# Attention of a fused block: half of the heads' probabilities transposed by DMA instead of TensorE, row transposes in their own PSUM bank, layernorm steps in other slots

## What is computed

```python
x = x + jnp.tanh(g_xattn[0]) * _L0_xattn_ref(_layernorm(x, axis=-1), ctx_1024, Wq, Wk, Wv, Wo, bo)
x = x + jnp.tanh(g_ffn[0]) * _L0_ffn_ref(_layernorm(x, axis=-1), router_w, w_gate, ...)
```

```python
scores = jnp.einsum('bhqd,bhkd->bhqk', q, k) * SCALE
scores = jnp.where(causal[None, None, :, :], scores, -jnp.inf)
probs = jax.nn.softmax(scores, axis=-1)
y = jnp.einsum('bhqk,bhkd->bhqd', probs, v)
```

## Time and profile before

| | us |
|---|---|
| median of 3 runs | 1925.9 (1924.12 to 1927.26) |
| the profiled execution | 1926.66 |
| its span in the trace | 1924.9 |
| attention, start of the span to the first expert matmul | 662.8 |
| experts | 1262.1 |

### The profile page before, as it was taken

One profiled execution on the slowest core, in us unless ns is written; L12 is line 12 of the kernel. 1 busy time (PEld: TensorE's weight loads), 2 busy tenths in 40 slices (PEclk: granted clock), 3 DMA queues, 4 the chain that ended last, 5 costly groups with the idle time before them and its releaser, 6 DMA issues.

```text
span 1924.9 us, 33464 instructions
## 1 busy us (share of the span) xinstructions
PE 1872.5 (97%) x11664; PEld 1588.0 (82%) x11664; DVE 1513.8 (79%) x3345; ACT 970.2 (50%) x2284; POOL 698.4 (36%) x939
## 2 busy tenths in 40 slices
PE   6999999999999899999999999999999999999999
PEld 6899998889999678888878888877888887888887
DVE  5888888888888887777788777787777778877776
ACT  4777777777777744243343333353334334423332
POOL 3132233232233533334433344353334453333330
PEclk9999999999999899999999999999999999999999
DMA  7565556656566231221123212114122112312111
GB/s 213 124 148 132 148 147 144 156 128 160 149 146 162 67 121 44 77 77 46 54 75 112 74 58 67 55 33 147 51 77 67 55 56 66 112 53 65 45 44 44
DMA packets 151494, 182.81 MB, mean 95 GB/s; under 512 B 11424, under 2 KB 115872, under 8 KB 151328
## 3 DMA queue, kind: packets, MB, share of 16 engines
q1 hardware_dynamic: 151328, 180.68, 33.4%
HBM read 111.43 MB, written 18.87 MB: 68 GB/s over the span
## 4 chain that ended last, share of the span: by engine, by line
PE 75%; DVE 13%; issue 5%; ACT 3%; POOL 3%; SPq 1%; DMA 1%; DVEq 0%; POOLq 0%; ACTq 0%
PE gate_up L1234 31%; PE down L1748 18%; PE bank L741 14%; PE probs_t L872 3%; PE scores L842 2%; DVE ops_lo L1091 2%; DVE acc L1599 2%; PE bank L731 1%; POOL hidden L1447 1%; DVE probs L673 1%; PE y L861 1%; PE y L859 1%; PE down L1727 1%; SPq L353 1%; DVE pt_lo L705 1%
## 5 line engine op out<-in xcount | busy, mean ns | idle before, releaser
L1234 PE MATMUL gate_up<-xo_hi,ops_hi 128*128 128x512 f32 x1120 | 440.0, 393 | 13.2 <-DVE hidden L1210 4.4
L1234 PE MATMUL gate_up<-xo_lo,ops_hi 128*128 128x512 f32 x1120 | 436.1, 389 | 0.0
L1234 PE MATMUL gate_up<-xo_hi,ops_lo 128*128 128x512 f32 x1120 | 436.1, 389 | 0.0
L1234 PEld LDWEIGHTS gate_up<-xo_hi,ops_hi 128*128 128x128 f32 x1120 | 210.2, 188 | 67.2 <-DVE gated L1210 9.6
L1599 DVE SCALAR_TENSOR_TENSOR acc<-down,scale,acc 128x512 f32<-128x512 f32 x320 | 238.1, 745 | 34.8 <-PE down L1748 34.4
L1748 PE MATMUL down<-d_hi,h_hi 128*128 128x512 f32 x640 | 249.1, 389 | 0.0
L1748 PE MATMUL down<-d_hi,h_lo 128*128 128x512 f32 x640 | 249.0, 389 | 0.0
L1748 PE MATMUL down<-d_lo,h_hi 128*128 128x512 f32 x640 | 249.0, 389 | 0.0
L1234 PEld LDWEIGHTS gate_up<-xo_lo,ops_hi 128*128 128x128 f32 x1120 | 210.2, 188 | 44.3
L1234 PEld LDWEIGHTS gate_up<-xo_hi,ops_lo 128*128 128x128 f32 x1120 | 210.3, 188 | 42.3
L1447 POOL TENSOR_TENSOR hidden<-hidden,gated 128x512 f32<-128x512 f32 x120 | 157.4, 1319 | 189.8 <-DVE hidden L1215 170.4
(11 more groups left out here) (179 smaller groups left out, 4586.2 us busy)
## 6 DMA issues: line engine op xcount, KB each, us to landing
g_raw<-in_w_gate SPq DMA_DIRECT2D x40, 512.0 KB, 3.9
u_raw<-in_w_up SPq DMA_DIRECT2D x40, 512.0 KB, 3.9
d_raw<-in_w_down SPq DMA_DIRECT2D x40, 512.0 KB, 3.7
k_stack<-k_hi SPq DMA_DIRECT2D x128, 128.0 KB, 2.6
q_stack<-q_hi SPq DMA_DIRECT2D x128, 128.0 KB, 2.6
c_in<-in_ctx_t SPq DMA_DIRECT2D x16, 512.0 KB, 3.8
x_in<-in_x SPq DMA_DIRECT2D x16, 512.0 KB, 3.8
k_stack<-k_lo SPq DMA_DIRECT2D x64, 128.0 KB, 2.6
```

Of the source, the lines that this page charges most:

```text
L1234: ins = pe.matmul(gu_ps[bank][:], ops[x][:, which, a, c, :], xo[y][:, b, c, :], start=(begins and c == 0 and i == 0), stop=(c == CH - 1 an ...
```

## The change

- Of each batch the even heads (`by_dma`) are no longer transposed by PE. ACT rounds their `probs` to float16 in SBUF (`halves[.., 0]`), POOL subtracts for the remainder (`halves[.., 1]`), both one slot behind the scores, and SP issues, two slots behind, one DMA that transposes all six 128x128 blocks into `turned`, a ring of four. The odd heads go through PE, ACT and DVE as before, three slots behind and through one bank; their results are written to `turned` too. The product with V is six slots behind instead of four.
- The scores' first matmul (queries 0 to 127) takes 128 keys instead of 256. The stacks lie in another order in SBUF, so that each of the 24 DMAs writes 4 KB in one piece instead of four of 1 KB.
- The bank set free, `rows_ps`, takes all row transposes. Those of y no longer wait for `q_lo`. The hat tile is transposed at once in slot 13 and evacuated once (`keep_hat`) instead of in four pieces.
- The layernorm steps stand in other slots (`LN_SLOT` 5 to 7, `XN_SLOT` 13 to 10, `MOMENTS_SLOT` 3 to 0, `STD_SLOT` 4 to 2). SP walks over slots as well: its loads, the stack DMAs (three in each of slots 5 to 12) and the turns are interleaved, and the store of x1 is issued in slot 0 of the next iteration.

```diff
-        return sb(f"q_stack{i}", [P, H, S], F32R), sb(f"k_stack{i}", [P, H, S], F32R)
+        return sb(f"q_stack{i}", [P, JH, C, S], F32R), sb(f"k_stack{i}", [P, JH, C, S], F32R)
...
-    RING = 4
+    RING, TURNED = 4, 4
     probs = [sb(f"probs{i}", [P, 3 * P]) for i in range(RING)]
-    pt_hi = [sb(f"pt_hi{i}", [P, 3 * P], F16) for i in range(2)]
-    pt_lo = [sb(f"pt_lo{i}", [P, 3 * P], F16) for i in range(2)]
+    halves = [sb(f"halves{i}", [P, 2, 3 * P], F16) for i in range(2)]
+    turned = [sb(f"turned{i}", [P, 2, 3, P], F16) for i in range(TURNED)]
...
-    sc_ps = [psum(f"scores{i}", [P, T, S]) for i in range(2)]
-    pt_ps = [psum(f"probs_t{i}", [P, D]) for i in range(2)]
+    sc_ps = [psum(f"scores{i}", [P, P + 3 * P]) for i in range(2)]
+    pt_ps = psum("probs_t", [P, D])
+    rows_ps = psum("rows_t", [P, D])
...
-    TR_LAG, PV_LAG = 2, 4
+    SPLIT_LAG, TURN_LAG, TR_LAG, PV_LAG = 1, 2, 3, 6
     GROUP_LAG = PV_LAG + JH
-    BANK_A, BANK_B = 0, 1
+    RES_LOAD, X_LOAD, C_LOAD, ROWS_LOAD = 2, 3, 14, 14
+    K_STACK, Q_STACK = (5, 6, 7, 8), (9, 10, 11, 12)
     K_SLOTS, K_EVAC = (0, 1, 2, 3), (2, 4)
-    X_SLOTS, X_EVAC, X_BANKS = (0, 2), (1, 3), (BANK_B, BANK_A)
+    X_SLOTS, X_EVAC = (0, 2), (1, 3)
     Q_SLOTS, Q_EVAC = (4, 5, 6, 7), (6, 8)
     V_SLOTS, V_EVAC, V_SPLIT = ((8, 9), (10, 11)), (10, 12), (11, 13)
-    Y_SLOTS, Y_EVAC, Y_BANKS = (8, 10), (9, 11), (BANK_B, BANK_A)
+    Y_SLOTS, Y_EVAC = (8, 10), (9, 11)
     O_SLOTS, O_EVAC = ((12, 13), (14, 15)), (14, 15)
-    LN_SLOT, C_SLOT, XN_SLOT = 5, 12, 13
-    RES_SLOT, MOMENTS_SLOT, STD_SLOT, HAT_SLOT = 6, 3, 4, 6
-    HAT_FIRST, HAT_T_SLOT = 4, H - C
+    LN_SLOT, C_SLOT, XN_SLOT = 7, 12, 10
+    RES_SLOT, MOMENTS_SLOT, STD_SLOT, HAT_SLOT = 6, 0, 2, 6
+    HAT_FIRST, HAT_T_SLOT, HAT_T_EVAC = 4, 13, 14
...
+    def scores_of(k, t):
+
+        return sc_ps[k % 2][:, P:2 * P] if t == 0 else sc_ps[k % 2][:, 2 * P:]
+
...
+            def turn(k):
+                wait(sp, pv_done, k - TURNED + 1)
+                sp.sem_inc(sp_passed, 1)
+                sp.wait_ge(p_lo_made, k // 2 + 1)
+                sp.dma_start(turned[k % TURNED][:].rearrange("p x t q -> p (x t) q"), halves[k // 2 % 2][:].rearrange("p x k -> p (x k)"),
+                             transpose=True).then_inc(p_turned[k // 2 % 2], DMA)
...
+                for s in range(H):
+                    if (bh := lagging(i, s, TURN_LAG)) and by_dma(bh[1]):
+                        turn(head(*bh))
+                    if s == 0 and has(i, -2):
+                        sp.wait_ge(x1_made, (i + -2).times(T, T))
+                        sp.dma_start(row(x1_v, i + -2), x_res[:]).then_inc(x1_stored, DMA)
...
+                    if s == RES_LOAD and has(i, -1):
+                        wait(sp, x1_stored, o.times(DMA))
+                        sp.dma_start(x_res[:], row(x_v, o)).then_inc(res_loaded, DMA)
+                    if s == ROWS_LOAD and hat_tile(i + 1) is not None:
+                        rows_again(hat_tile(i + 1))
+                    if s == X_LOAD and has(i, 2):
+                        sp.wait_ge(xt_done, ln.times(T))
+                        sp.dma_start(x_in[:], row(x_v, ln)).then_inc(x_loaded, DMA)
...
+                    if s in Q_STACK and has(i, 1):
+                        j = Q_STACK.index(s)
+                        if j == 0:
+                            sp.wait_ge(q_lo_made, n.times(2, 2))
                         stack(q_stack[par], j, 0, q_hi).then_inc(stacked[par][j], DMA)
                         stack(q_stack[par], j, 1, q_lo).then_inc(stacked[par][j], DMA)
                         stack(q_stack[par], j, 2, q_hi).then_inc(stacked[par][j], DMA)
...
+                    if s == C_LOAD and has(i, 3):
+                        sp.wait_ge(c_lo_made, far.times(1))
+                        sp.dma_start(c_in[:], row(c_v, far)).then_inc(c_loaded, DMA)
...
+                    if (bh := lagging(i, s, SPLIT_LAG)) and by_dma(bh[1]):
+                        k = head(*bh)
+                        m = k // 2
+                        pool.wait_ge(p_hi_made, m + 1)
+                        pool.tensor_tensor(halves[m % 2][:, 1, :], probs[k % RING][:], halves[m % 2][:, 0, :],
+                                           ALU.subtract).then_inc(p_lo_made, 1)
...
+                    if (bh := lagging(i, s, SPLIT_LAG)) and by_dma(bh[1]):
+                        k = head(*bh)
+                        m = k // 2
+                        if m >= 2:
+                            act.wait_ge(p_turned[m % 2], DMA * (m // 2))
+                        act.wait_ge(probs_made, k + 1)
+                        act.copy(halves[m % 2][:, 0, :], probs[k % RING][:]).then_inc(p_hi_made, 1)
+                    if (bh := lagging(i, s, TR_LAG)) and not by_dma(bh[1]):
+                        k = head(*bh)
+                        act.wait_ge(pt_done, k // 2 + 1)
+                        wait(act, pv_done, k - TURNED + 1)
+                        act.copy(turned[k % TURNED][:, 0].rearrange("p t q -> p (t q)"), pt_ps[:, 0:3 * P]).then_inc(pt_hi_made, 1)
...
-                        wait(dve, pt_done, i.times(H, s - RING + 1))
+                        k = head(i, s)
+                        if k >= RING and by_dma(k):
+                            dve.wait_ge(p_lo_made, (k - RING) // 2 + 1)
+                        elif k >= RING:
+                            dve.wait_ge(pt_done, (k - RING) // 2 + 1)
...
+                    if (bh := lagging(i, s, TR_LAG)) and not by_dma(bh[1]):
+                        k = head(*bh)
+                        dve.wait_ge(pt_hi_made, k // 2 + 1)
+                        p_hi, p_lo = (turned[k % TURNED][:, x].rearrange("p t q -> p (t q)") for x in range(2))
+                        dve.tensor_tensor(p_lo, pt_ps[:, 0:3 * P], p_hi, ALU.subtract).then_inc(pt_lo_made, 1)
...
-                        if has(i, 1) and t == 0:
-                            pe.wait_ge(q_lo_made, n.times(2, 2))
-                        elif has(i, 1):
-                            pe.wait_ge(v_rest_made, n.times(T, 1))
-                        else:
-                            wait(pe, x1_made, o.times(T, (0, 1 - T)[t]))
-                        transpose_rows(lambda c: y_chunk(o, t, c), bank[Y_BANKS[t]]).then_inc(yt_done, 1)
+                        if is_end(i):
+                            pe.wait_ge(x1_made, o.times(T, (0, 1 - T)[t]))
+                        elif t == 1:
+                            pe.wait_ge(yt_lo_made, o.times(T, 1))
+                        transpose_rows(lambda c: y_chunk(o, t, c), y_bank(i, t)).then_inc(yt_done, 1)
...
-                        wait(pe, max_made, i.times(H, s - 1))
+                        wait(pe, max_made, head(i, s) - 1)
                         pairs = slice(0, 3 * DH)
                         for t in range(T):
-                            ins = pe.matmul(sc_ps[s % 2][:, t, :], q_stack[par][pairs, s, tile(t)],
-                                            k_stack[par][pairs, s, :], start=True, stop=True)
+                            keys = slice(0, P * (t + 1))
+                            ins = pe.matmul(scores_of(head(i, s), t), q_stack[par][pairs, s % JH, s // JH, tile(t)],
+                                            k_stack[par][pairs, s % JH, s // JH, keys], start=True, stop=True)
...
-                        pe.wait_ge(pt_lo_made, b.times(H, h + 1))
+                        n_head = head(b, h)
+                        if by_dma(n_head):
+                            pe.wait_ge(p_turned[n_head // 2 % 2], DMA * (n_head // 4 + 1))
+                        else:
+                            pe.wait_ge(pt_lo_made, n_head // 2 + 1)
+                        p_hi, p_lo = turned[n_head % TURNED][:, 0], turned[n_head % TURNED][:, 1]
...
+                    if (bh := lagging(i, s, TR_LAG)) and not by_dma(bh[1]):
+                        j = head(*bh)
+                        pe.wait_ge(probs_made, j + 1)
+                        wait(pe, pt_lo_made, j // 2)
                         for k in range(3):
-                            ins = pe.transpose(pt_ps[h % 2][:, tile(k)], probs[h % RING][:, tile(k)], ident[:])
+                            ins = pe.transpose(pt_ps[:, tile(k)], probs[j % RING][:, tile(k)], ident[:])
                         ins.then_inc(pt_done, 1)
                     units(i, s)
+                    if s == HAT_T_SLOT and hat_tile(i) is not None:
+                        k = hat_tile(i)
+                        pe.wait_ge(x_hat_made, k + 1)
+                        transpose_rows(lambda c: x_hat[:, k % T, c * P:(c + 1) * P], rows_ps).then_inc(hat_t_done, 1)
```

179 lines of the change are left out of this document (81 added, 98 removed).

## The result

The changed kernel takes **1907.0 us** (median of 4 runs, 1905.8 to 1910.3) against 1925.3 us before (4 runs, 1924.1 to 1927.3): a ratio of 0.990, 95% interval 0.989 to 0.992. It is 18 us faster where 39 were forecast; 1907.0 lies inside the range. The profiled execution took 1910.3 us, with a span of 1908.6.

A forecast was written before the change was run, and what follows sets the result against it. PE was taken to bound the kernel, busy 97% of the span. Five batches by 2.54, eight hat batches by 3.64 and 1.2 for batch 0, less 4 at the end, give 39.0 us: 1887 us, range 1866 to 1944.

The forecast's parts named there:

- The transposes: On PE, removing three transposes for each of 8 heads saves 0.28 us each, 2.24 us a batch.
- the sum: All terms added over the whole kernel: 39.0 us gained from 1926.66, giving 1887 us as median.
- The narrower scores: On PE, a 128-column first score matmul saves 0.02 us a head, 0.3 us a batch (1.0 gained to 1.8 lost).
- the best case: Narrow score matmul on PE costs half of one with 256 columns, 0.06 us; 1.0 us gained a batch.
- The rival "dear": Narrow score matmuls cost 0.23 us each on PE, a batch loses 1.8 us, about 1920 us; chance 0.15.
- The bank of its own: Row transpose of y no longer waits on PE for q_lo: 1.1 us saved in each of eight hat batches.
- all fit into 35.6 and are priced at nothing: DVE 29.5, ACT 29.2, POOL 18 us (21 with hat tile) fit a 35.6 us batch, so cost nothing.
- The hat batches: Batches 4 to 11, with a hat tile: 3.64 us gained in each of eight, 29.1 us in all.
- The queue: On SP, a turn's issue takes 1 to 1.5 us; SP sets the pace only from 2.25 us.
- the heavy rival: A turn holds SP for 3.7 us, 47.2 us of issues a batch, 2050 us in all; chance 0.20.
- the 2.56 that were given: Issue time in us per turn on SP from which the kernel is slower than before.
- The end: Batches 14 and 15: POOL's remainders queue behind its wait for x_t; 4 us lost (gain 3 to loss 12).

The follow-up runs named there:

- h4: f2 with the first score matmul of each head taking all 256 keys again (wide scores): 1895.3 us.
- g1: Changed kernel, but the row transpose of y's first tile waits for q's remainder again, as with a shared bank: 1914.1 us.
- f1: Changed kernel plus one wait: POOL's remainder in slot 11 waits for DVE's two layernorm scalings of slot 10: 1899.3 us.
- i1: h5 (with its first expert sum in slot 12) plus the hat tile's moments in slot 3 and u_raw loaded in slot 14: 1886.7 us.
- h5: f2 without f1's wait: scalings in slot 11, POOL's third part of V there waiting for them: 1888.9 us.
- i4: i1 with each turn issued as two DMAs of three blocks instead of one of six: 1980.5 us.
- e2: Changed kernel with POOL's first sum for the experts in iteration 14 moved from slot 8 to slot 12: 1901.0 us.
- f2: f1 with the first expert sum moved to slot 12, as in e2: 1891.5 us.

## Why the prediction was half right

**The transposes: right.** A slot without them takes 2.00 to 2.01 us, with them 2.28 to 2.29; 0.28 times 8 is the 2.24 us of the sum.

**The narrower scores: right in sign, a quarter in size.** A pair takes 0.238 instead of 0.242 us, and a plain batch gains 0.08 us (h4) instead of 0.3: some 3 us less over the kernel than the sum had. The narrow matmul is at half, as in the best case, but its neighbour pays for it. The rival "dear" is out.

**The bank of its own: right.** The sum had 1.1 us in eight batches, 8.8 us, and slot 8 takes 2.60 us in all batches now. What the sum couldn't know is that with the shorter slots and without the bank q's remainder would have been late in 13 batches, which g1 against f1 prices at 14.8 us.

**The step that failed: "all fit into 35.6 and are priced at nothing".** That is true of the sums of busy time (DVE 29.8, ACT 28.8, POOL 17.3 us of 36.8) and says nothing about where a moved instruction stands. The change moved DVE's scalings from slot 13 to slot 10, directly ahead of a remainder that PE needs two slots later, and the prediction didn't cost that move at all. With the collision it costs 0.98 us in each plain batch (36.77 against 35.78 in i1, in which the scalings take 1.02 us): 0.73 through POOL's remainder, as f1 shows, and 0.25 through the place, as h5 shows.

The prediction weighed the rule for this, by the Trainium skill (SBUF — State Buffer, Who interferes with whom), only for instructions with two SBUF inputs, and gave it no price. The same section also names `tensor_scalar` in its two-port mode as one that shuts out GpSimd and is shut out, and says "Issue order, not op shape, decides who blocks." The traces agree in that either can be the one that is held: 1.00 us alone, 1.73 or 1.00 as POOL comes 0.52 or 0.54 us behind the start, 3.74 beside two POOL rows, and 1.23 instead of 0.92 us for POOL when it came later. Two things they don't show: whether these two instructions ran in that mode, and what counts as the issue. The row of the second scaling begins 0.46 us behind the first in both cases, ahead of POOL's, and all the same it is the one held at 0.52 us. The kernel before had shown it too, had one asked for the duration of that line and what POOL did beside it (DVE, then POOL, batch 2):

```profile
150.74 2.66 DVE L597 TENSOR_SCALAR x_in<-x_in,mv,rstd 128x512 f32<-128x512 f32 x2
```

```profile
149.42 2.39 POOL L445 TENSOR_TENSOR c_lo<-c_in,c_hi 128x1024 fp32r<-128x1024 f32 x1 [4.19 <-ACT c_hi L479]
151.76 1.35 POOL L453 TENSOR_TENSOR v_parts<-v_rest,v_parts 128x512 bf16<-128x512 f32 x1
```

**The hat batches** came to 37.2 to 37.9 us instead of 36.1. Besides the hole above they have a wait of 0 to 0.7 us in slot 4, by the load of x_hat, since the moments stand in slot 0. That move wasn't costed either. With the moments in slot 3 and the scalings in slot 11 (i1) they take 36.2 us, against the 36.1 of the forecast.

**The queue: right, and its rival was nearer than the prediction had it.** A turn's issue takes 1.25 us, in the 1 to 1.5 that were taken; in batches 2 and 3 it landed after 2.8 to 4.6 us (medians 3.2 and 2.8), and the rings' share is 0.81 to 0.93 in the batches shown. i4 is the heavy rival made real. At 2.5 us a turn the prediction's count gives 17.6 + 20 = 37.6 us a batch, just under the 38.1 of before; it measured 40.5 to 44.0, with SP's issues filling 38 to 41 us of each, some of them 1.6 to 2.6 us long instead of 0.6 or 1.25. So the kernel is slower than before already at 2.5 us a turn, under the 2.56 that were given; how far under, no run shows.

**The end: the right mechanism, too small.** Remainders behind the sum's wait for `x_t`, DVE held at `probs`: named word for word, with 2 to 3 us and 4 in the sum. It measured 10.6 in the profiled execution, 6 to 10 in the four others with the same order. The wait was read off the row of before, as if the load kept its place. Before, the sum began 615.9 - 589.7 = 26.2 us into batch 14; in the changed kernel it begins 590.0 - 560.9 = 29.1 us into it, because the load of `x_t` goes out 3.3 us later (582.35 - 560.90 = 21.5 us into the batch, before 607.83 - 589.65 = 18.2), behind stacks and turns on SP. The slip in counting slots made it look smaller as well: the 618.4 that were taken for DVE's next use of `probs` belong to slot 13, while it is head 12, whose maximum begins at 616.75, that takes over the buffer of head 8. By the same subtraction the wait is 2.6 us and not 0.9, before any slot gets shorter. DVE meanwhile gets to the `probs` in question earlier, by its shorter slots. The clock and the turn behind the weight loads, a wait of 6 us for PE, come on top; neither was in the sum. e2 gives 6 us back by moving one sum.

**What the sum missed is accounted for.** From the changed kernel, step by step: 7.7 us by POOL's wait (f1), 7.9 by the first sum (f2), 2.6 by the scalings in slot 11 (h5), 2.2 by the moments and the late load together (i1; the last two steps are each near the spread of the runs). i1 is at 1886.7 us, the 1887 of the forecast. It is not the same kernel, though: the forecast was for the order that the change brought, and there it was wrong. That the two agree to a microsecond is partly luck: i1's batches 2 to 13 take 2 us more than forecast and its experts 2 more, its end takes 4 less and its start 1.5 less.

What stays open: how much of the end's remaining waits is the rings and how much SP's queue, which no run here takes apart; what decides which of the two engines is held; and why the experts take 0.3 to 2.3 us more in all the changed kernels.
